# Four graph layers on one core: the output projection in rounded halves, two low parts on GpSimd, the first z on VectorE, and new orders on all engines

## The reference

```python
h = jnp.maximum(_layernorm(x), 0.0)
# L0: 8 heads; q, k, v = h @ w_qkv; softmax over neighbours (adj); o = heads @ w_proj + b_proj
x = x + (o + layernorm(o) * gamma + beta)
h = jnp.maximum(_layernorm(x), 0.0)
# L1: rel = adj.T * (q k^T), rows divided by their norm
x = x + rel @ v
h = jnp.maximum(_layernorm(x), 0.0)
# L2: hw = h @ W; att = softmax(leaky_relu(s1 + s2) * adj)
x = x + elu(att @ hw + beta * hw)
h = jnp.maximum(_layernorm(x), 0.0)
# L3
x = x + (adj @ h) @ weight + bias
```

## Time and profile before

| | us |
|---|---|
| median of 3 runs | 1482.62 (1481.49 to 1482.86) |
| the profiled execution | 1483.83 |
| its span in the trace | 1482.0 |
| TensorE busy | 1448.4 |
| VectorE busy | 1296.7 |
| ScalarE busy | 1169.9 |
| GpSimd busy | 606.9 |

### The profile page before, as it was taken

How to read it: one execution, slowest core, us unless ns; L and a number is a source line. 1 busy time by engine, 2 the same in 40 slices (tenths; PEclk the granted TensorE clock), 3 DMA queues, 4 the chain that set the end, 5 groups by cost and what they waited for, 6 DMA issues and landing times.

```text
span 1482.0 us, 47177 instructions
## 1 busy us (share of the span) xinstructions
PE 1448.4 (98%) x15880; PEld 1375.0 (93%) x15880; DVE 1296.7 (87%) x5774; ACT 1169.9 (79%) x2948; POOL 606.9 (41%) x977
## 2 busy tenths in 40 slices
PE   6999999999999999999999999999999999999996
PEld 5899999999999999999999999999999999999985
DVE  3889988998989889889889889889889889889884
ACT  4788878878878878878878888888888878878763
POOL 3244434434434434444444444444444344344342
PEclk9999999999999999999999999999999999999997
DMA  3000101101000001000000010010010010000000
GB/s 111 16 16 23 30 17 30 30 18 30 24 23 30 22 25 30 19 28 30 17 31 30 16 31 30 16 31 30 17 30 30 16 30 30 17 30 30 11 21 30
DMA packets 38111, 39.87 MB, mean 27 GB/s; under 512 B 2416, under 2 KB 37488, under 8 KB 37872
## 3 DMA queue, kind: packets, MB, share of 16 engines
q1 hardware_dynamic: 37872, 36.84, 8.4%
HBM read 20.05 MB, written 16.78 MB: 25 GB/s over the span
## 4 chain that ended last, share of the span: by engine, by line
PE 95%; DVE 3%; issue 1%; POOL 0%; DMA 0%; ACT 0%; SPq 0%; POOLq 0%; DVEq 0%; ACTq 0%
PE bank L313 31%; PE mid L313 12%; PE bank L320 7%; PE bank L348 5%; PE mid L357 5%; PE bank L369 4%; PE mid L440 4%; PE mid L461 4%; PE bank L493 4%; PE bank L329 4%; PE bank L373 4%; PE mid L512 4%; PE mid L348 2%; PE mid L329 2%; PE mid L470 1%
## 5 line engine op out<-in xcount | busy, mean ns | idle before, releaser
L541 ACT ACTIVATE probs<-masked,neg_max 128x128 f32<-128x128 f32 x1024 | 312.0, 391 | 0.2 <-DVE neg_max L715 0.2
L715 DVE CUSTOM_DVE_ANT_0 masked<-mid,mask 128x128 f32<-128x128 f32 x1024 | 230.9, 287 | 18.1 <-issue 12.3
L905 POOL TENSOR_TENSOR rstd<-var_eps,minus_half 128x2 f32<-128x2 f32 x320 | 222.0, 694 | 25.1
L934 POOL TENSOR_TENSOR x3b<-x_up,b_out_less 128x512 f32<-128x512 f32 x64 | 82.3, 1287 | 283.1 <-DVE x L854 283.1
L903 POOL TENSOR_TENSOR var_eps<-mean_var,eps 128x2 f32<-128x2 f32 x320 | 62.9, 197 | 291.4 <-DVE mean_var L709 291.2
L705 DVE BATCH_NORM_STATS2 stats<-x 128x6 f32<-128x256 f32 x384 | 142.8, 413 | 3.5 <-DMA x<-in_x 3.5
L320 PE MATMUL bank<-w_proj_sb,o_t 128*128 128x256 f32 x512 | 121.0, 379 | 0.1
L348 PE MATMUL bank<-ident,probs 128*128 128x128 f32 x768 | 115.5, 273 | 1.9 <-ACT probs L541 1.0
L798 DVE SCALAR_TENSOR_TENSOR x<-mid,inv_norm,x 128x256 f32<-128x256 f32 x128 | 56.0, 480 | 70.1 <-PE mid L512 70.1
L914 POOL TENSOR_TENSOR inv_norm<-sum_sq,minus_half 128x2 f32<-128x2 f32 x64 | 66.7, 1043 | 119.8 <-DVE sum_sq L773 119.8
L938 POOL TENSOR_TENSOR xb<-x,b_proj_beta 128x512 f32<-128x512 f32 x64 | 81.5, 1273 | 60.7 <-DVE o_res L862 60.7
(11 more groups left out here) (142 smaller groups left out, 5373.4 us busy)
## 6 DMA issues: line engine op xcount, KB each, us to landing
x<-in_x SPq DMA_DIRECT2D x64, 256.0 KB, 2.9
out_x<-x SPq DMA_DIRECT2D x64, 256.0 KB, 3.2
w_qkv_sb<-in_w_qkv SPq DMA_DIRECT2D x1, 768.0 KB, 4.9
w_q_sb<-in_w_q SPq DMA_DIRECT2D x1, 256.0 KB, 4.8
w_k_sb<-in_w_k SPq DMA_DIRECT2D x1, 256.0 KB, 5.0
w_v_sb<-in_w_v_t SPq DMA_DIRECT2D x1, 256.0 KB, 5.7
w_proj_sb<-in_w_proj SPq DMA_DIRECT2D x1, 256.0 KB, 5.9
w_gat_x<-in_w_gat SPq DMA_DIRECT2D x1, 256.0 KB, 6.4
```

Source lines behind the costliest of these rows:

```text
L541: last = act.activation(probs[:, r, s], masked[:, r, s], ACT.Exp, scale=-1.0, bias=neg_max[:, r, s:s + 1])
L715: last = dve.tensor_tensor_reduce(out=masked[:, r, s], in0=mid[:, r, s * N:(s + 1) * N], in1=mask[:], scale=1.0, scalar=LARGE, op0=ALU.add ...
L905: pool.tensor_tensor(rstd[:, k], var_eps[:, k], minus_half[:], ALU.pow).then_inc(ln_rstd[k], 1)
```

## The change

1. **o in halves.** ScalarE rounds `o_t` into `o_t_hi`, GpSimd subtracts it from `o_t` to get `o_t_lo`, `w_proj` is split in the set-up, and the four float32 matmuls become the 12 matmuls of `product`.
2. **The low part of h_t1 on GpSimd.** ScalarE writes `h_t1_full` first and then `h_t1_hi`, both from PSUM; GpSimd subtracts the two. VectorE's `relu_lo(1, ...)` is gone.
3. **z0 on VectorE.** `normalize(0, ...)` takes the place of `shift0` and of ScalarE's two activations.
4. **Orders and banks.** All four engines have new orders and the PSUM blocks new banks. Several stages move to the neighbouring step.

```diff
-        SPLIT = [(w_v_sb[:], w_v_p)]
+        SPLIT = [(w_v_sb[:], w_v_p), (w_proj_sb[:], w_proj_p)]
...
                 if on[2]:
-                    pe.wait_ge(o_norm_ready, done(p2))
-                    bank_free(pe, (o_norm_ready, p2, 1), (probs_t_ready[0], p2, 1))
-                    rows_f32(halves(o_bank), lambda b, c: o_t[:, b, c], w_proj_sb).then_inc(o_psum, 1)
...
+                    pe.wait_ge(o_lo_ready, done(p2))
+                    bank_free(pe, (max_ready[0], p1, 1), (ln_sum_ready, p2, 1), (probs_t_ready[0], p2, 1))
+                    for b in range(2):
+                        last = product(o_bank[:, b * D:(b + 1) * D], o_t_p, w_proj_p,
+                                       lambda a, c: a[:, b, c], lambda a, c: a[:, c])
+                    last.then_inc(o_psum, 1)
...
+                    act.wait_ge(o_norm_ready, done(p2))
+                    wait_before(act, o_psum, p2)
+                    act.activation(o_t_p[0][:], o_t[:], ACT.Copy).then_inc(o_hi_ready, 1)
...
-                    for b in range(2):
-                        last = act.activation(z[0][:, b], x0[:, i0, b], ACT.Identity, bias=shift0[:, b:b + 1],
-                                              scale=rstd[:, 0, b:b + 1])
-                    last.then_inc(z_ready[0], 1)
...
-                if on[3]:
-                    relu_lo(1, p3, z1_bank)
-                if on[0]:
-                    dve.wait_ge(ln_rstd[0], done(p0))
-                    wait_before(dve, z_ready[0], p0)
-                    dve.scalar_tensor_tensor(shift0[:], mean_var[:, 0, :, 0], -1.0, rstd[:, 0], ALU.mult, ALU.mult)\
-                       .then_inc(shift0_ready, 1)
...
+                if on[0]:
+                    normalize(0, p0, x0[:, i0])
...
+                if on[3]:
+                    pool.wait_ge(h1_full_ready, done(p3))
+                    pool.wait_ge(h_hi_ready[1], done(p3))
+                    pool.tensor_tensor(flat(h_t[1][1]), flat(h_t1_full), flat(h_t[1][0]).bitcast(f32), ALU.subtract)\
+                        .then_inc(h_lo_ready[1], 1)
+                if on[2]:
+                    pool.wait_ge(o_hi_ready, done(p2))
+                    pool.tensor_tensor(o_t_p[1][:], o_t[:], o_t_p[0][:].bitcast(f32), ALU.subtract).then_inc(o_lo_ready, 1)
```

More of the change, by code:

```diff
@@ L115, in gnn_stack @@
         o_t = sb("o_t", [128, 2, C, N])
+        o_t_p = parts("o_t", [128, 2, C, N])
         o = sb("o", [128, 2, D])
@@ L403, in step @@
                 if on[1]:
+                    pe.wait_ge(h_lo_ready[0], done(p1))
+                    bank_free(pe, (hw_ready, p5, 2), (h_lo_ready[2], p5, 1), (max_ready[2], p2, 1))
+                    columns(q_bank, w_qkv_p, 0, h_t[0]).then_inc(q_psum, 1)
+                if on[3]:
+                    pe.wait_ge(z_ready[1], done(p3))
+                    bank_free(pe, (hw_ready, p5, 2), (v1_ready, p4, 1), (g_ready, p4, 1))
+                    transposes(z1_bank, z[1]).then_inc(h_t_psum[1], 1)
@@ L404, in step @@
+                if on[4]:
+                    pe.wait_ge(v1_ready, done(p4))
+                    pe.wait_ge(rel_ready, done(p4))
+                    bank_free(pe, (k_ready, p1, 1), (probs_t_ready[3], p2, 1), (att_t_ready, p6, 1))
+                    for b in range(2):
+                        last = pe.matmul(rel_v_bank[:, b * D:(b + 1) * D], rel[:, b], v1[:, b], start=True, stop=True)
+                    last.then_inc(rel_v_psum, 1)
+                if on[1]:
                     pe.wait_ge(q_ready, done(p1))
@@ new lines, in step @@
+                if on[5]:
+                    act.wait_ge(e_max_ready, done(p5))
+                    wait_before(act, att_norm_ready, p5, 2)
+                    for b in range(2):
+                        act.activation(att[:, b], e_mask[:, b], ACT.Exp, bias=e_neg_max[:, b:b + 1],
+                                       accum_out=att_sum[:, b:b + 1]).then_inc(att_ready, 1)
+                if on[1]:
+                    act.wait_ge(max_ready[0], done(p1))
+                    wait_before(act, probs_t_psum[0], p1)
+                    exps(0).then_inc(probs_ready[0], 1)
+                    act.wait_ge(v0_psum, done(p1))
+                    wait_before(act, heads_psum, p1)
+                    act.activation(v0[:].rearrange("p b h d -> p (b h d)"), v_bank, ACT.Copy).then_inc(v0_ready, 1)
@@ L659, in step @@
-                if on[0]:
-                    act.wait_ge(shift0_ready, done(p0))
-                    wait_before(act, h_t_psum[0], p0)
-                    for b in range(2):
-                        last = act.activation(z[0][:, b], x0[:, i0, b], ACT.Identity, bias=shift0[:, b:b + 1],
-                                              scale=rstd[:, 0, b:b + 1])
-                    last.then_inc(z_ready[0], 1)
-            run(act, step, [(1, copy_fold)])
+                    act.activation(flat(g_t), g_bank, ACT.Copy).then_inc(g_ready, 1)
@@ L669, in _ @@
+                if on[0]:
+                    act.wait_ge(h_t_psum[0], done(p0))
+                    wait_before(act, v0_psum, p0)
+                    act.activation(flat(h_t[0][0]), z0_bank, ACT.Relu).then_inc(h_hi_ready[0], 1)
+            run(act, step, [(0, copy_fold)])
         @block.vector
```

469 lines of the change are left out of this document (221 added, 248 removed).

## The result

The changed kernel takes 1474.47 us (median of 4 runs, 1472.32 to 1474.85). The kernel before, measured beside it, takes 1482.05 (4 runs, 1480.25 to 1482.86). The ratio is 0.9943, with a 95% interval of 0.9931 to 0.9955: 0.6% faster. The prediction said 1476. The profiled execution took 1474.63 us, its span is 9.2 us shorter than before.

What follows compares the result with a forecast made beforehand. TensorE's blocks, end to end, were taken to bound the kernel. From 1483.83 us profiled, −7.7 for the steps and +1.0 for the ends gave 1477.1; runs' median 1.2 lower, so 1476. Likeliest case 1467 to 1482; 8-in-10 range 1465 to 1484.

Steps and rivals of the forecast that it cites:

- What bounds the kernel: Steady middle: TensorE is busy 100 us of 100, no block waits, so the step is the sum of its blocks.
- o in halves: TensorE's o block: 12 matmuls take 1.40 us in place of 1.72, shorter by 0.32, between 0.29 and 0.33.
- The new order: TensorE's step: one added change of tiling, one exit and one entry, costs 0.20 us, between 0.12 and 0.22.
- the full saving: TensorE's step, read without the rule that a tiling change drains TensorE: it would win the full 0.32 us.
- blocks cost the same wherever they stand except beside heads and scores: TensorE's matmul blocks: moving them changes no length, except beside heads and scores, which use the array in tiles.
- The step: Scores to scores: 22.21 us, between 22.12 and 22.26, from 22.33; 0.12 shorter, 7.7 us over 64 pairs.
- Slack: Operands of TensorE's blocks come in time: q_t 0.6 us to spare, x4 0.9, o_t_lo 2.3, h_t1_lo 2.1.
- One sign: List of waits in the new profile: none of TensorE's entries has 60 times.
- The ends: Fill and drain together: +1 us, between −2 and +4, from 1.7 more in the drain and −0.7 in the fill.
- VectorE held by GpSimd: Rival, chance 0.13: wide GpSimd subtractions hold VectorE before x4; TensorE waits 0.4 us per step, time 1499.

Runs made afterwards that it cites:

- experiments 1 and 2: 1 is b_halves, the kernel before with only o in halves, 1471.0 us; 2 is a_o_f32, the changed kernel with o in float32, 1493.69 us.
- b_halves: The kernel before with only the output projection o in rounded halves, old order kept: 1471.0 us, ratio 0.9922.
- Experiment 3: The kernel before with z1's transposes put between the two halves of heads, one more change of tiling: 1506.58 us, ratio 1.0166.
- a_o_f32: The changed kernel with o back to four float32 matmuls, without the copy and subtraction only o needs: 1493.69 us, ratio 1.0079.
- experiment 5: The changed kernel with GpSimd making o_t_lo twice, first into a tile nothing reads: 1478.6 us, ratio 0.9976.
- a_pad8: The changed kernel with one unused tile of 8 bytes where shift0 stood, no instruction changed: 1471.39 us.

## Why the prediction was right

- **What bounds the kernel: right.** TensorE is busy 100 us of 100 in the middle of every version, and the step is the sum of its blocks.
- **o in halves: right, a little too large.** 1.40 was forecast, between 1.39 and 1.43, and 1.427 measured; the saving is 0.30 in place of 0.32, and experiments 1 and 2 show it in both orders (0.31 and 0.30).
- **The new order: right.** 0.20 was forecast; experiments 1 and 2 give 0.19 and 0.17 from two sides, and the records put 0.09 at the entry into heads and 0.10 at the exit towards y_t. The rule of the Trainium skill, "TensorEngine Tiling (Array Packing)", Key Properties, that a mode change drains TensorE, was weighed against the full saving. The trace agrees: a step would be 22.01 without that cost, and `b_halves`, in the old order, has just that. Experiment 3 shows that the price isn't one number. One sentence of the prediction is wrong, that blocks cost the same wherever they stand except beside heads and scores: before, q takes 1.428 behind hw, and k 1.505 behind y_t. It does no harm, because the narrow block in front gives back what the product takes.
- **The step: 22.20, forecast 22.21.** 57 steady steps give 7.6 us where 7.7 was summed with 64. The two errors, 0.02 too much saving and 0.01 to 0.03 too much cost, cancel, so the sum is better than its terms.
- **Slack: right at each place.** `q_t` 0.60 forecast and 0.60 measured; `o_t_lo` ready at 3.2 and 3.06; x4 at 7.1 and 6.87 (0.1 of the difference is a reading: `o_t` takes 0.69 by its row, and 0.6 was put down); o's start at 5.5 and 5.48. One sign did not come: the waits do have an entry of TensorE with 60 times, the load for scores with 61. It awaits nothing, and stood in the list before with 64.
- **The ends: the least certain term, and off.** +1 was forecast, from 1.7 more in the drain less 0.7 in the fill. In the two profiled executions they are −1.5: −1.8 in the first six intervals, +0.7 at the first scores, −0.4 in the drain. By the medians, which differ by 7.6 us, just what the steady steps give, they are about 0. All lie inside the bounds of −2 to +4. The −1.8 is o's saving in six intervals: the five kernels with the new order, o in halves and no extra work have 105.5 to 105.9 us there, and `a_o_f32`, the same order with o in float32, has 107.3, near the 107.5 of before. In the old order the halves make it 112.1 (`b_halves`). So the new order costs 0.19 in each of 57 steps, 10.6 us, and buys back 6.4 in the fill. The +0.7 belongs to no order: over all kernels the first scores starts between 19.7 and 21.8 us. In the drain the granted clock covers the answer. The last y starts 75.2 us after the last scores before and between 74.8 and 76.0 in the same five kernels, so 1.7 more is not what came. The low part of o does lie on that path, as experiment 5 shows (2.1 us up to the last y for one more of 1.3). What the new order gives back there, and at which block, I did not take apart; that stays open.
- **The clock at the ends was left out.** The kernel before ran 32 times beside the experiments. Eight executions with a mean granted clock of 0.995 took 1481.5 us in the mean, five with 0.991 took 1484.2. So the ends of one execution can't be read closer than 2 or 3 us, and that the forecast 1476 came within 1.5 of 1474.47 is in part luck.
- **VectorE held by GpSimd: real, but not in its place.** Experiment 5 shows it on shift, 155 to 554 ns. The Trainium skill, "SBUF — State Buffer", "SBUF: two separate sides", says that VectorE and GpSimd share a port pair under an exclusive lock, which a VectorE operation with two SBUF inputs needs. The trace agrees in this: shift ends when `o_t_lo` does. Beside a narrow root it does not: there shift takes 0.15 us, though it starts inside the root. In the changed kernel masked rows and moments stand beside the two subtractions, and those keep their pace (masked rows 286 ns in the mean and 287 before, the statistics 415 and 413); VectorE's room of 1.1 us at z0 (x4 ready at 6.87, z0 at 8.01) was not touched. The same thing runs the other way: GpSimd's roots take 753 ns in the mean, and 694 before.

`b_halves` has 0.9922 (0.9907 to 0.9937) against 0.9943 (0.9931 to 0.9955). It is 3.5 us ahead of the changed kernel in the medians, with intervals that just overlap, and level with `a_pad8`. By the step, 22.01 against 22.20, it should be 11 us ahead; it loses 6.4 us of that in the fill (112.1 against 105.7). Its profiled execution (1468.34) lies 2.7 us below its other runs, and I can't say why.

## What to carry to other kernels

Where one engine is busy all the time, add up the distances between the starts of its blocks, and price a change of order by the same rows: a cheaper operation and a dearer order can hide each other (−0.30 and +0.18 us here), and only undoing each alone shows it. A slack found in the steady step says nothing about fill and drain, where every new link lies on the path: test the two with separate readings. Before explaining a difference of 2 or 3 us, look whether tiles have moved in SBUF, and whether fill and drain had the same granted clock in both profiles.

## What the runs showed of the hardware that was not expected

- **The pace of matmuls depends on where tiles lie in SBUF.** With 8 bytes more ahead of them, the 12 matmuls of y behind scores take 1.478 in place of 1.524 us, g 1.418 in place of 1.440, and v0 1.430 in place of 1.410. The step goes from 22.20 to 22.17, the median from 1474.47 to 1471.39 us. 57 steps make 1.5 us of these 3.1; the rest lies in the ends. The intervals (0.9931 to 0.9955, 0.9913 to 0.9939) overlap by a little, so the blocks show it more firmly than the time.
- **GpSimd's narrow operations are held too.** The root of two columns takes 753 ns in the mean, and 694 before. In the changed kernel 118 of the 320 roots run at the same time as one of VectorE's z and take 854 ns in the mean; the other 202 take 693. Before, 3 did. Timeline of VectorE and GpSimd in the changed kernel:

```profile
720.89 1.35 DVE L725 TENSOR_SCALAR z<-x,mean_var,rstd 128x256 f32<-128x256 f32 x4
...
721.41 0.87 POOL L903 TENSOR_TENSOR rstd<-var_eps,minus_half 128x2 f32<-128x2 f32 x1
```

- **The price of a change of tiling is not one number.** One more entry and exit costs 0.19 us where heads moves between hw and y_t, and 0.34 per step in all where z1's transposes stand between two halves of heads.
